# A graph attention layer and a routed feed-forward layer on one core: the attention row of the edge loops held in PSUM, and the dense softmax of the second layer put in another order

## The chip, the cores and the metric

The kernel runs on one core of a Trainium2 chip. The metric is the device time of one execution in microseconds. The profile is of one execution; its engines are TensorE (PE, with its weight loads as PEld), VectorE (DVE), ScalarE (ACT), GpSimd (POOL) and the queue of SyncE (SPq), which issues most plain DMAs.

## The reference

There are N = 625 nodes with 768 features and 10,625 edges. After a layer norm two branches are added to x, and then a routed feed-forward layer with its own layer norm:

```
x = x + gnn(xn, src, dst) + mixer(xn)
x = x + ffn(layernorm(x))
gatv2: fs = x @ Ws + bs ; fd = x @ Wd + bd
       e = leaky_relu(fs[src] + fd[dst], 0.2) ; logits = sum(e * attn)      # per edge and head
       alpha = softmax of the logits over the edges of one dst
       out = elu(sum over edges of alpha * fs[src])
gnn:   h = layer_norm(gatv2(x) with 8 heads + x) * w + b
       layer_norm(gatv2(h) with 1 head) * lno_w + lno_b
mixer: q, k, v of 12 heads of 64 ; relu features of 256 ; num / den ; @ proj_w.T + proj_b
ffn:   sigmoid gate, top 2 of 8 experts, each silu(x w1) * (x w3) @ w2, and one shared expert
```

## The kernel before

Node rows lie in T = 5 tiles of P = 125; D = 768 is six chunks (KC) of 128 for TensorE, or two halves (HALF = 384). Edges lie in ET = 84 tiles of 128. There is no planner: each engine has its own program in `build`, the order is written out by hand, and semaphores join them.

**Stages.** First the layer norm and the products of layer 1 (`products`, drained by `products_out`), written as tables of rows to DRAM. Then edge loop 1, a dense softmax of layer 1 (`dense(0)`), the products of layer 2, edge loop 2, the dense softmax of layer 2 (`dense(1)`), the gate, the shared expert and the routed jobs.

**An edge loop** (`edges` on GpSimd, `edges_first` and `edges_second` on VectorE). For tile t GpSimd issues three indirect DMAs: it gathers the rows of fs for tile t+5 (`gather_src`, L571) and of fd (`gather_dst`, L577) into a ring of G = 5 slots, and scatters the logits of tile t into a dense matrix in DRAM (`scatter`, L582). It waits for `edge_done` of tile t before the three. VectorE adds the two gathered rows (`edge_sum`, L998, 769 or 776 columns), multiplies relu of the sum by the attention row `rows[:, 2, :]`, which lies in SBUF (`weigh`, L1010 in loop 1, L1039 in loop 2), sums it and adds the linear part (`total`, L1019 and L1044, which gives `edge_done`). Loop 1 also makes one-hot rows (`hot`, L1005) and sums by head with a reduction (L1014); TensorE counts edges with them into banks 0 to 6 of PSUM (L1492). In loop 2 TensorE and ScalarE work on the mixer (`MIX_STEPS`), whose kv products use banks 4 and 5, its num products banks 6 and 7 (`mix_bank`), and the rest banks 0 to 3. From tile 64 of loop 2 on VectorE puts one step of the mixer's projection behind each tile (`project`): five divisions (L1061), two weight splits (`weights_lo`, L916), five low halves of transposes (`transposed_lo(2, t)`, L911) and ten drains of products 8 and 9 (L927). When the five transposes are done, SyncE loads x once more into `b1` (L478).

**The dense softmax of layer 2.** SyncE loads the logits of the five tiles; VectorE finds the maxima, ScalarE takes Exp, VectorE multiplies by the edge counts (`probs`). TensorE transposes each tile of probabilities (L1513), ScalarE copies it out (L738), TensorE multiplies it with fs (L1527, 20 matmuls a tile, into banks 4 and 5 or 6 and 7). Then VectorE does for one tile after another: scale (L1160), min (L1169), max (L1174), the sum with Exp from ScalarE (L746, L1185), and `finish(c)`: statistics (L888, L890), 1/std (L894, behind the square root of ScalarE, L660), two instructions for the norm's rows (L902, L904), the sum with the residual `x2` (L1208), statistics again, and the normalised tile `xf` (L898) for the gate. `transposes(3, t)` brings xf to TensorE (L1454), L668 and L911 split it in a high and a low half, `gate_product(t)` is 18 matmuls (L1436 to L1438). `x2` had got its `x` in five additions (L1146), behind which `xagain_used` lets SyncE load the first expert pieces.

Of the kernel before, what the change touches and what calls it, by code (L numbers as in the profile page):

```python
# [66 lines left out]
def build(nc, x, src, dst, W1s, b1s, W1d, b1d, attn1, ln1_w, ln1_b, Wos, bos, Wod, bod, attno, lno_w,  # L67
          lno_b, qkv_wT, qk_bcols, v_brow, proj_wT, proj_b, proj_matT, gate_wT, gate_bias, moe_w, out):
    ctx = ExitStack()
    with ctx:  # L70
# [200 lines left out]
        xagain_loaded, xagain_used = sem("xagain_loaded"), sem("xagain_used")  # L271
# [90 lines left out]
        AGG_LAG, COPY_LAG, NORM_LAG, ELU_LAG, OUT_LAG = 2, (3, 0), (4, 2), (5, 2), (6, 2)  # L362
# [6 lines left out]
        def _(sp):  # L369
# [123 lines left out]
            sp.wait_ge(xagain_used, 1)  # L493
# [155 lines left out]
        def _(act):  # L649
# [60 lines left out]
            def dense(l):  # L710
# [14 lines left out]

                if l == 1:
                    for u in range(T):
                        exps(u)
                for u in range(H * T + OUT_LAG[l] + (2 if l == 0 else 0)):
                    if l == 0 and u < H * T:  # L730
                        exps(u)
                    v = u - COPY_LAG[l]
                    if 0 <= v < H * T:
                        act.wait_ge(pt_full[l], v + 1)
                        if v >= PT_SLOTS:
                            act.wait_ge(agg_full[l], v - PT_SLOTS + 1)
                        m = v % PT_SLOTS
                        act.copy(pt[:, m * N:(m + 1) * N], pt_psum(v)).then_inc(pt_copied[l], 1)  # L738
                    if l == 0 and v == H * T - 1:
                        weights_hi([4])  # L740
                        transposed_hi(1, 0)
                    c, rest = divmod(u - ELU_LAG[l] + 1, H)
                    if rest == 0 and 1 <= c <= T:
                        elu_m = (elu_m_t, elu_m2)[l][:, :]
                        act.wait_ge(elu_min[l], c)
                        act.activation(elu_m, elu_m, ACT.Exp).then_inc(elu_exp[l], 1)  # L746
                        if l == 1:
                            ln_sqrt(2, c - 1)
                            if c >= 3:
                                transposed_hi(3, c - 3)  # L750
                            ln_sqrt(3, c - 1)
                        elif c == T:
                            transposed_hi(1, 1)
                    c, rest = divmod(u - OUT_LAG[l], H)
                    if l == 0 and rest == 0 and 1 <= c <= T:
                        ln_sqrt(1, c - 1)
# [14 lines left out]
            for n, (kind, r, h, i) in enumerate(MIX_STEPS):  # L771
# [23 lines left out]
                else:  # L795
                    last = act.copy(mix_out[:, :, 2 * r + h, :], ps[0:P, b, 0:T * (MD + 1)].rearrange("p (t d) -> p t d", t=T))
# [79 lines left out]
        def _(dve):  # L876
# [123 lines left out]
            def edges_first():  # L1000
# [63 lines left out]
            def project(i):  # L1064
# [18 lines left out]
            def dense(l, dest):  # L1083
                H = HL[l]
                DH = D // H
                elu_o, elu_m = (elu_o_t[:, :], elu_m_t[:, :]) if l == 0 else (elu_o2[:, :], elu_m2[:, :])
# [44 lines left out]
                for u in range(H * T + OUT_LAG[l] + (2 if l == 0 else 0)):  # L1131
                    if l == 0 and u < H * T:
# [8 lines left out]
                    if l == 1 and u == 0:  # L1141
                        dve.memset(at[:, :, :, N:TP].bitcast(F32), 0.0)
                        dve.wait_ge(xagain_loaded, 16 * len(PARTS))
                        dve.wait_ge(mm_used, 50)
                        for t in range(T):
                            last = dve.tensor_tensor(x2[:, t, :], x2[:, t, :], b1[:, t, :], ALU.add)  # L1146
                        last.then_inc(xagain_used, 1)
                        dve.wait_ge(xagain_used, 1)
                    c, rest = divmod(u - NORM_LAG[l] + 1, H)
                    if l == 0 and rest == 0 and c == T:  # L1150
                        weights_lo([4])
                    if rest == 0 and 1 <= c <= T:
# [6 lines left out]
                        if H == 1:  # L1159
                            last = dve.tensor_scalar(elu_o.rearrange("p (a d) -> p a d", a=2), pv, rden[:, c, 0:1], None, ALU.mult)  # L1160
                        else:
                            for b in range(2):
                                last = dve.tensor_tensor(
                                    elu_o[:, b * HALF:(b + 1) * HALF].rearrange("p (h d) -> p h d", d=DH),
                                    pv[:, b, :].rearrange("p (h d) -> p h d", d=DH),
                                    rden[:, c, 4 * b:4 * b + 4].unsqueeze(2).to_broadcast([P, 4, DH]), ALU.mult)
# [3 lines left out]
                        if l == 0:  # L1170
# [647 lines left out]
```

## Time and profile before

| | us |
|---|---|
| median of 3 runs | 1414.26 (1414.21 to 1416.88) |
| the profiled execution | 1414.86 |
| its span (first to last instruction) | 1413.1 |
| DVE busy | 943.8 (67%) |
| PE busy | 1024.6 (73%) |
| POOL busy | 619.8 (44%) |
| ACT busy | 564.1 (40%) |
| mean granted TensorE clock | 0.859 |

The span is the profiled execution less 1.8 us ahead of its first and behind its last instruction. The shares of busy time are means over stages of very different kinds, so what an engine's share says of a stage has to be read in that stage. A DMA-issuing instruction of POOL is shown with the time that it takes to be issued, not with the time of the transfer.

### The profile page before, as it was taken

Reading aid. Unit: us, or ns where it says so; the run is one execution under the profiler, and the core shown is the slowest. Engines: PE = TensorE matmul, PEld = TensorE weight load, DVE = VectorE, ACT = ScalarE, POOL = GpSimd, SP = SyncE. Lnnn points to the kernel's source line nnn. Section 1 sums busy time; section 2 is a strip of 40 time slices with the busy share of each in tenths; the row PEclk is TensorE's granted clock in tenths of the full one; section 3 lists DMA queues with packets and bytes.
Section 4 is the critical chain, followed back from the end, with each engine's and each line's share of the span. In section 5 each row is a group of like instructions: output and inputs, shape, how many; then the busy total and the mean of one; then the engine's idle time right before and its main releaser. Section 6 shows DMA issues by size and latency. Waiting matters only on the chain.

```text
span 1413.1 us, 15862 instructions
## 1 busy us (share of the span) xinstructions
PE 1024.6 (73%) x5499; PEld 855.4 (61%) x5499; DVE 943.8 (67%) x1678; ACT 564.1 (40%) x735; POOL 619.8 (44%) x581
## 2 busy tenths in 40 slices
PE   5974455545551777798999999518267998999991
PEld 5963333333331676797777778418245997888881
DVE  6548777778774787544444444475488655999993
ACT  3314333333422788310444343310034423777770
POOL 0037777777772000004777777787400000333330
PEclk9999787677875788899999999858687799999995
DMA  9856666666666550237777766758412125999986
GB/s 337 344 190 185 200 196 197 199 200 195 196 193 175 140 137 25 72 103 252 220 220 219 231 183 185 256 164 236 127 71 66 57 101 222 388 408 403 400 353 186
DMA packets 85033, 290.85 MB, mean 206 GB/s; under 512 B 15970, under 2 KB 37768, under 8 KB 84341
## 3 DMA queue, kind: packets, MB, share of 16 engines
q0 software_dynamic: 34656, 145.11, 34.3%
q1 hardware_dynamic: 46822, 130.71, 27.1%
q10 hardware_dynamic: 3488, 14.16, 2.5%
q8 instruction: 40, 0.66, 0.2%
q14 instruction: 27, 0.22, 0.1%
HBM read 258.31 MB, written 31.62 MB: 205 GB/s over the span
## 4 chain that ended last, share of the span: by engine, by line
POOL 30%; PE 29%; DVE 13%; issue 12%; DMA 12%; ACT 4%; SPq 1%; DVEq 0%; ACTq 0%; POOLq 0%
POOL dense_logits L582 11%; POOL ring_s L571 10%; POOL ring_d L577 9%; PE ps L1436 9%; PE ps L1437 9%; PE ps L1438 9%; DMA ring_d<-table_dst,dst_i 7%; ACT de L724 2%; DVE ring_s L998 2%; DVE ring_s L1010 1%; DMA dl_b<-dense_logits 1%; DVE stats L888 1%; DMA y_in<-y_rows 1%; PE ps L1527 1%; DMA dl_a<-dense_logits 1%
## 5 line engine op out<-in xcount | busy, mean ns | idle before, releaser
L998 DVE TENSOR_TENSOR ring_s<-ring_s,ring_d 128x776 f32<-128x776 f32 (+1 forms) x168 | 162.1, 965 | 255.9 <-DMA ring_d<-table_dst,dst_i 255.9
L571 POOL DMA_INDIRECT ring_s<-table_src,src_i x168 | 173.6, 1033 | 328.0 <-DVE fd_stage L927 268.7
L1492 PE MATMUL ps<-hot_s,hot_d 128*125 128x512 f16 (+1 forms) x840 | 177.7, 374 | 163.3 <-DVE hot_s L1005 162.9
L1492 PEld LDWEIGHTS ps<-hot_s,hot_d 128*125 128x125 f16 x840 | 112.0, 173 | 229.2 <-DVE hot_s L1005 173.4
L582 POOL DMA_INDIRECT dense_logits<-logits,cell_i x168 | 204.4, 1217 | 51.4 <-issue 50.6
L577 POOL DMA_INDIRECT ring_d<-table_dst,dst_i x168 | 171.4, 1020 | 76.6 <-issue 50.6
L698 ACT ACTIVATE hot_d<-iota_h,dst_bias 128x626 f16<-128x626 f16 x84 | 68.5, 816 | 220.4 <-PE ps L1492 220.3
L610 POOL COPY gather_i<-lst 128x1 int32 (+1 forms) x16 | 7.4, 463 | 245.0 <-DVE lst L1356 149.9
L1436 PE MATMUL ps<-wp,at 128*125 128x384 f32 x300 | 105.3, 351 | 11.1 <-DVE xt L927 4.1
L1437 PE MATMUL ps<-wp,at 128*125 128x384 f32 x300 | 104.0, 347 | 0.0
L1438 PE MATMUL ps<-wp,at 128*125 128x384 f32 x300 | 103.6, 345 | 0.0
L1243 DVE TENSOR_TENSOR we<-eraw,we 128x1536 fp32r<-128x1536 f32 x50 | 86.4, 1756 | 12.7 <-ACT we L814 11.8
L1527 PE MATMUL ps<-fs,dpt 125*125 125x96 f32 (+1 forms) x500 | 92.9, 342 | 0.0
L1527 PEld LDWEIGHTS ps<-fs,dpt 125*125 125x125 f32 x500 | 75.3, 216 | 13.5 <-issue 2.5
L1568 PE MATMUL ps<-xt,mix_w 128*128 128x313 f32 (+1 forms) x288 | 80.3, 436 | 2.0 <-issue 1.7
L1039 DVE SCALAR_TENSOR_TENSOR ring_d<-ring_s,rows 128x768 f32<-128x768 f32 x84 | 80.7, 961 | 0.0
L1014 DVE TENSOR_REDUCE head_sum<-ring_s 128x8 f32<-128x768 f32 x84 | 80.1, 953 | 0.0
L1010 DVE SCALAR_TENSOR_TENSOR ring_s<-ring_s,rows 128x768 f32<-128x768 f32 x84 | 80.0, 952 | 0.0
L1513 PE MATMUL ps<-ident,de 125*125 125x125 f32 x200 | 37.6, 330 | 55.5 <-DVE den L1118 34.4
L1243 DVE TENSOR_TENSOR we<-raw,we 128x1536 fp32r<-128x1536 f32 x44 | 75.8, 1752 | 0.0
L814 ACT CAST we<-eraw 128x1536 fp32r<-128x1536 f32 x50 | 72.2, 1481 | 5.6 <-PE ps L1438 5.6
L1568 PEld LDWEIGHTS ps<-xt,mix_w 128*128 128x128 f32 x288 | 54.6, 192 | 27.6 <-ACT mix_qp L769 5.2
(248 smaller groups left out, 2341.9 us busy)
## 6 DMA issues: line engine op xcount, KB each, us to landing
eraw<-in_moe_w_dram SPq DMA_DIRECT2D x50, 768.0 KB, 6.7
raw<-in_moe_w_dram SPq DMA_DIRECT2D x44, 768.0 KB, 7.3
dense_logits<-neg ACTq DMA_DIRECT2D x1, 12288.0 KB, 44.5
mix_w<-in_qkv_wT_dram SPq DMA_DIRECT2D x18, 384.0 KB, 6.1
dl_a<-dense_logits SPq DMA_DIRECT2D x2, 2187.5 KB
dl_b<-dense_logits SPq DMA_DIRECT2D x2, 2187.5 KB
y_in<-y_rows SPq DMA_DIRECT2D x5, 672.0 KB
ring_s<-table_src,src_i POOLq DMA_INDIRECT x168, 4.2
```

The source lines that it names most:

```text
L571: pool.indirect_dma_start(out=ring_s[:, j, 0:WL[l]], out_offset=None, in_=table_src[l], in_offset=bass.IndirectOffsetOnAxis(ap=src_i[:, t: ...
L577: pool.indirect_dma_start(out=ring_d[:, j, 0:WL[l]], out_offset=None, in_=table_dst[l], in_offset=bass.IndirectOffsetOnAxis(ap=dst_i[:, t: ...
L582: pool.indirect_dma_start(out=dense_logits[l], out_offset=bass.IndirectOffsetOnAxis(ap=cell_i[:, t:t + 1], axis=0), in_=logits[:, t, 0:HL[ ...
L998: dve.tensor_tensor(ring_s[:, j, 0:WL[l]], ring_s[:, j, 0:WL[l]], ring_d[:, j, 0:WL[l]], ALU.add).then_inc(z_ready[l], 1)
L1010: dve.scalar_tensor_tensor(out=v, in0=v, scalar=0.0, in1=rows[:, 2, :], op0=ALU.max, op1=ALU.mult).then_inc(mul_ready[0], 1)
L1243: dve.tensor_tensor(we[:, 2 * m + 1, part], src, we[:, 2 * m, part].bitcast(F32), ALU.subtract).then_inc(up_lo if q < 4 else w2_lo, 1)
L1436: pe.matmul(o, lt(0), r(0), start=start, stop=False)
L1437: pe.matmul(o, lt(0), r(1), start=False, stop=False)
L1438: return pe.matmul(o, lt(1), r(0), start=False, stop=stop)
L1492: last = pe.matmul(ps[0:P, b, o:o + s1 - s0], hot_d[:, j, c * P:(c + 1) * P], hot_s[:, j, s0:s1], start=start and (n <= 5 or n == 9), stop ...
L1527: last = pe.matmul(o, pt[:, m * N + s * P:m * N + (s + 1) * P], fs[:, s, col:col + w], start=s == 0, stop=s == T - 1)
L1568: last = pe.matmul(ps[:, b, 0:c1 - c0], mix_w[:, 1 - m, k, s * 128:(s + 1) * 128], xt_v[:, k, c0:c1], start=k == 0, stop=k == KC - 1)
```

## The change

1. The attention row times 0.8 is written to PSUM (`att_ps`, the last 768 columns of banks 6 and 7). In loop 1 only its last 512 columns, in bank 7, are used from there, and `weigh` is two instructions, of 256 columns (attention in SBUF) and of 512 (attention in PSUM). In loop 2 the whole row is read from PSUM by the one `weigh`.
2. Banks 6 and 7 are no longer used by the mixer: its num products go to other columns of the banks of kv (`NUM_AT`), and the transposes of stage 2 use banks 4 and 5 only: `transposes(2, t)` now waits for the low half of tile t-1, where it waited for t-2.
3. The second addition of x is gone. The two biases (proj_b, lno_b) are added by TensorE, two matmuls of one row ahead of each product of q = 8 and 9, and the drain adds `b1` (x loaded again) in place of a bias row; it waits for `xagain_loaded`. SyncE loads the first expert pieces when `mm_used` is 50.
4. The dense softmax of layer 2 has loops of its own: ScalarE makes max(scale*v, 0) from PSUM, VectorE the min in one instruction, and VectorE works on tile c and on the norms of tile c-1 in turn. Per tile it issues one scale-and-min, one sum, two instructions for the norm and the residual (before: two and one more), the two statistics, two reciprocals and the normalisation. `transposed_lo(3, t)` is three rounds behind; `copy_probs(4)` of ScalarE stands behind Exp of tile 0 and ahead of that tile's square root.

```diff
+        att_ps = ps[:, 6:8, :].rearrange("p a b -> p (a b)")[:, 1024 - D:1024]
-                b = (0 if n == 3 else 4) + 2 * (t % 2)
+                b = 2 * (t % 2) if n == 3 else 4
...
-            sp.wait_ge(xagain_used, 1)
+            sp.wait_ge(mm_used, 50)
...
+                    for v in range(PT_SLOTS):
+                        copy_probs(v)
+                    for c in range(T + 1):
+                        if c < T:
+                            act.wait_ge(elu_min[l], c + 1)
+                            pv = ps[0:P, 4 + 2 * (c % 2):6 + 2 * (c % 2), 0:HALF]
+                            act.activation(elu_o2[:, :].rearrange("p (a d) -> p a d", a=2), pv, ACT.Relu,
+                                           scale=rden[:, c, 0:1]).then_inc(elu_max[l], 1)
+                            act.activation(elu_m2[:, :], elu_m2[:, :], ACT.Exp).then_inc(elu_exp[l], 1)
+                        if c == 0:
+                            copy_probs(PT_SLOTS)
+                        if c >= 3:
+                            transposed_hi(3, c - 3)
+                        if c >= 1:
+                            ln_sqrt(3, c - 1)
+                        if c < T:
+                            ln_sqrt(2, c)
...
-                dve.tensor_scalar(rows[:, 2, :], rows[:, 2, :], 0.8, None, ALU.mult).then_inc(att_scaled, 1)
+                if l == 0:
+                    dve.tensor_scalar(att_ps[:, D - 512:D], rows[:, 2, D - 512:D], 0.8, None, ALU.mult)
+                    dve.tensor_scalar(rows[:, 2, 0:D - 512], rows[:, 2, 0:D - 512], 0.8, None, ALU.mult).then_inc(att_scaled, 1)
+                else:
+                    dve.tensor_scalar(att_ps, rows[:, 2, :], 0.8, None, ALU.mult).then_inc(att_scaled, 1)
...
-                    v = ring_s[:, t % G, 0:D]
-                    dve.scalar_tensor_tensor(out=v, in0=v, scalar=0.0, in1=rows[:, 2, :], op0=ALU.max, op1=ALU.mult).then_inc(mul_ready[0], 1)
+                    for cols, att in ((slice(0, D - 512), rows[:, 2, 0:D - 512]), (slice(D - 512, D), att_ps[:, D - 512:D])):
+                        v = ring_s[:, t % G, cols]
+                        last = dve.scalar_tensor_tensor(out=v, in0=v, scalar=0.0, in1=att, op0=ALU.max, op1=ALU.mult)
+                    last.then_inc(mul_ready[0], 1)
...
-                    dve.scalar_tensor_tensor(out=ring_d[:, j, 0:D], in0=ring_s[:, j, 0:D], scalar=0.0, in1=rows[:, 2, :],
+                    dve.scalar_tensor_tensor(out=ring_d[:, j, 0:D], in0=ring_s[:, j, 0:D], scalar=0.0, in1=att_ps,
...
-                    products_out(8 + q, x2, 3, "proj", tiles=(t,))
+                    dve.wait_ge(xagain_loaded, 16 * len(PARTS))
+                    u = 5 * (8 + q) + t
+                    dve.wait_ge(mm_full, u + 1)
+                    dve.tensor_tensor(x2[:, t, q * HALF:(q + 1) * HALF], ps[0:P, u % 4, 0:HALF],
+                                      b1[:, t, q * HALF:(q + 1) * HALF], ALU.add).then_inc(mm_used, 1)
...
+                for c in range(T + 1):
+                    if c < T:
+                        dve.wait_ge(agg_full[1], c + 1)
+                        pv = ps[0:P, 4 + 2 * (c % 2):6 + 2 * (c % 2), 0:HALF]
+                        dve.tensor_scalar(elu_m2[:, :].rearrange("p (a d) -> p a d", a=2), pv, rden[:, c, 0:1], 0.0,
+                                          ALU.mult, ALU.min).then_inc(elu_min[1], 1)
+                    if c >= 1:
+                        o = gnn[:, c - 1, :]
+                        ln_rstd(2, c - 1)
+                        after(dve.scalar_tensor_tensor(out=o, in0=o, scalar=mv[:, c - 1, 0:1], in1=rows[0:P, 0, :],
+                                                       op0=ALU.subtract, op1=ALU.mult))
+                        after(dve.scalar_tensor_tensor(out=x2[:, c - 1, :], in0=o, scalar=rstd[:, c - 1:c], in1=x2[:, c - 1, :],
+                                                       op0=ALU.mult, op1=ALU.add))
+                        ln_stats(c - 1, x2[:, c - 1, :])
+                    if c >= 3:
+                        transposed_lo(3, c - 3)
+                    if c < T:
+                        dve.wait_ge(elu_exp[1], c + 1)
+                        dve.wait_ge(elu_max[1], c + 1)
+                        dve.scalar_tensor_tensor(out=gnn[:, c, :], in0=elu_m2[:, :], scalar=-1.0, in1=elu_o2[:, :],
+                                                 op0=ALU.add, op1=ALU.add).then_inc(out_ready[1], 1)
+                        dve.wait_ge(out_ready[1], c + 1)
+                        ln_stats(c, gnn[:, c, :])
+                    if c >= 1:
+                        ln_rstd(3, c - 1)
+                        normalise(c - 1, x2[:, c - 1, :], xf[:, c - 1, :]).then_inc(ln_done, 1)
...
-                back = (4, 1, 2, 2)[n]
+                back = (4, 1, 1, 2)[n]
...
+                    if q >= 8:
+                        for r in (3, 1):
+                            pe.matmul(ps[0:P, u % 4, 0:HALF], ones_row[:, :], rows[0:1, r, (q - 8) * HALF:(q - 7) * HALF],
+                                      start=r == 3, stop=False)
...
+NUM_AT = 2 * (MD + 1)
-    if kind == "kv":
+    if kind in ("kv", "num"):
         return 4 + h
-    if kind == "num":
-        return 6 + h
```

## Rows read from the trace of the kernel before

**Rows 1.** Busy time by stretch: edge loop 1, edge loop 2 (columns in the row's order: stretch, length, PE, PEld, DVE, ACT, POOL, clock, DMA share, GB/s).

```profile
100.00:435.00 335.00, 176.14 (x830) 110.89 (x830) 259.56 (x417) 124.89 (x167) 257.18 (x243) 0.77 0.67 192
664.00:1010.00 346.00, 278.92 (x1566) 228.37 (x1566) 180.35 (x355) 108.61 (x237) 271.84 (x242) 0.89 0.70 207
```

**Rows 2.** Groups of POOL in loop 1, stretch 104 to 436.

```profile
L582 POOL DMA_INDIRECT dense_logits<-logits,cell_i x84 | 102.0, 1214 | 25.8 <-issue 25.0 <-DVE logits L1019 0.8
```

**Rows 3.** Groups of POOL in loop 2, stretch 664 to 1010.

```profile
L582 POOL DMA_INDIRECT dense_logits<-logits,cell_i x84 | 102.4, 1219 | 25.6 <-issue 25.6
L577 POOL DMA_INDIRECT ring_d<-table_dst,dst_i x79 | 84.9, 1074 | 24.1 <-issue 24.1
L571 POOL DMA_INDIRECT ring_s<-table_src,src_i x79 | 84.6, 1071 | 28.9 <-issue 22.3 <-DVE logits L1044 6.6
```

**Rows 4.** Timeline of loop 1 (start, length, engine, line).

```profile
205.95 0.97 DVE L998 TENSOR_TENSOR ring_s<-ring_s,ring_d 128x776 f32<-128x776 f32 x1 [1.04 <-DMA ring_d<-table_dst,dst_i]
206.44 1.33 POOL L582 DMA_INDIRECT dense_logits<-logits,cell_i  x1 [0.30 <-issue]
```

**Rows 5.** Timeline of loop 2: POOL and DVE at three places.

```profile
665.58 0.96 DVE L1039 SCALAR_TENSOR_TENSOR ring_d<-ring_s,rows 128x768 f32<-128x768 f32 x1
665.78 1.57 POOL L577 DMA_INDIRECT ring_d<-table_dst,dst_i  x1 [0.30 <-issue]
...
936.04 2.55 DVE L916 TENSOR_TENSOR wp<-wraw,wp 128x2304 fp32r<-128x2304 f32 x1
936.36 3.07 POOL L571 DMA_INDIRECT ring_s<-table_src,src_i  x1 [0.30 <-issue]
...
979.22 1.73 POOL L577 DMA_INDIRECT ring_d<-table_dst,dst_i  x1 [0.30 <-issue]
```

**Rows 6.** Groups of DVE by form in the dense softmax of layer 2, 1038 to 1097.4.

```profile
L888 DVE BATCH_NORM_STATS2 stats<-gnn 125x6 f32<-125x384 f32 x10 | 5.1, 552 | 0.2
L904 DVE SCALAR_TENSOR_TENSOR gnn<-gnn,rstd,rows 125x768 f32<-125x768 f32 x5 | 5.1, 1019 | 0.2
...
L1160 DVE TENSOR_SCALAR elu_o<-ps,rden 125x768 f32<-125x768 f32 x5 | 5.1, 1018 | 3.1 <-PE ps L1527 3.0
...
L898 DVE TENSOR_SCALAR xf<-xt,mv,rstd 125x768 f32<-125x768 f32 x5 | 3.4, 680 | 0.2
...
L894 DVE RECIPROCAL rstd<-std 125x1 f32<-125x1 f32 x10 | 1.6, 164 | 3.6 <-ACT std L660 3.6
```

**Rows 7.** Timeline from the dense softmax to the shared expert: first DVE, then PE.

```profile
1038.58 1.02 DVE L1160 TENSOR_SCALAR elu_o<-ps,rden 125x768 f32<-125x768 f32 x1 [2.96 <-PE ps L1527]
...
1045.84 6.62 PE L1527 MATMUL ps<-fs,dpt 125*125 125x384 f32 x20
1060.56 1.48 PE L1454 MATMUL ps<-ident,xf 125*128 125x125 f32 x6 [8.10 <-ACT dpt L738]
...
1084.97 1.51 PE L1454 MATMUL ps<-ident,xf 125*128 125x125 f32 x6 [6.57 <-DVE xf L898]
...
1101.82 0.37 PE L1436 MATMUL ps<-gate_w_hi,at 128*125 128x8 f32 x1 [1.86 <-DVE at L911]
...
1109.40 0.61 PE L1436 MATMUL ps<-at,we 128*128 128x314 f32 x1
```

**Rows 8.** Group of DVE whose second input lies in PSUM, whole span.

```profile
L1365 DVE TENSOR_TENSOR silu<-silu,ps 128x314 f32<-128x314 f32 x4 | 1.9, 472 | 0.0
```

**Rows 9.** Timeline near loop 2's end: last projection product, last drain.

```profile
997.16 0.34 PE L1438 MATMUL ps<-wp,at 128*125 128x384 f32 x1
...
1007.34 0.55 DVE L927 TENSOR_TENSOR xt<-ps,rows 125x384 f32<-125x384 f32 x1
```

**Rows 10.** Groups of ACT in the same stage, 1028 to 1097.

```profile
L660 ACT ACT_TABLE_LOAD x5 | 6.4, 1283 | 0.1
...
L746 ACT ACTIVATE elu_m<-elu_m 125x768 f32<-125x768 f32 x5 | 4.2, 843 | 12.9 <-DVE elu_m L1169 12.9
L738 ACT COPY dpt<-ps 125x625 f32<-125x625 f32 x5 | 3.4, 672 | 2.3 <-PE ps L1513 2.3
```

More of the change, by code:

```diff
@@ L731, in dense @@
+                    return
+                for u in range(H * T + OUT_LAG + 2):
+                    if u < H * T:
                         exps(u)
-                    v = u - COPY_LAG[l]
+                    v = u - COPY_LAG
                     if 0 <= v < H * T:
[L734 to L738, printed above, removed]
@@ L739, in dense @@
-                    if l == 0 and v == H * T - 1:
+                        copy_probs(v)
+                    if v == H * T - 1:
                         weights_hi([4])
                         transposed_hi(1, 0)
-                    c, rest = divmod(u - ELU_LAG[l] + 1, H)
+                    c, rest = divmod(u - ELU_LAG + 1, H)
                     if rest == 0 and 1 <= c <= T:
-                        elu_m = (elu_m_t, elu_m2)[l][:, :]
                         act.wait_ge(elu_min[l], c)
[L746 to L752, printed above, removed]
+                        act.activation(elu_m_t[:, :], elu_m_t[:, :], ACT.Exp).then_inc(elu_exp[l], 1)
+                        if c == T:
@@ L753, in dense @@
                             transposed_hi(1, 1)
-                    c, rest = divmod(u - OUT_LAG[l], H)
-                    if l == 0 and rest == 0 and 1 <= c <= T:
+                    c, rest = divmod(u - OUT_LAG, H)
+                    if rest == 0 and 1 <= c <= T:
                         ln_sqrt(1, c - 1)
@@ L795, in _ @@
                 else:
-                    last = act.copy(mix_out[:, :, 2 * r + h, :], ps[0:P, b, 0:T * (MD + 1)].rearrange("p (t d) -> p t d", t=T))
+                    last = act.copy(mix_out[:, :, 2 * r + h, :], ps[0:P, b, NUM_AT:NUM_AT + T * (MD + 1)].rearrange("p (t d) -> p t d", t=T))
                 last.then_inc(mix_used, 1)
@@ L1130, in dense @@
                         probs(u)
-                for u in range(H * T + OUT_LAG[l] + (2 if l == 0 else 0)):
-                    if l == 0 and u < H * T:
+                    second()
+                    return
+                for u in range(H * T + OUT_LAG + 2):
+                    if u < H * T:
                         c, h = divmod(u, H)
@@ L1140, in dense @@
                             joined(c + 1)
[L1141 to L1150, printed above, removed]
+                    c, rest = divmod(u - NORM_LAG + 1, H)
+                    if rest == 0 and c == T:
                         weights_lo([4])
@@ L1199, in dense, with second @@
                         normalise_rows(c - 1, b1[:, c - 1, :]).then_inc(ln_done, 1)
-            def finish(c):
-                o = gnn[:, c, :]
-                ln_stats(c, o)
-                ln_rstd(2, c)
-                after(normalise_rows(c, o))
-                after(dve.tensor_tensor(x2[:, c, :], x2[:, c, :], o, ALU.add))
-                if c >= 2:
-                    transposed_lo(3, c - 2)
-                ln_stats(c, x2[:, c, :])
-                ln_rstd(3, c)
-                normalise(c, x2[:, c, :], xf[:, c, :]).then_inc(ln_done, 1)
+            def second():
+                dve.wait_ge(mm_used, 50)
+                dve.memset(at[:, :, :, N:TP].bitcast(F32), 0.0)
+                dve.wait_ge(probs_ready[1], T)
+                after(dve.tensor_scalar(rden[:, :, 0:1], den[:, :, 0:1], 1e-30, None, ALU.max))
+                after(dve.reciprocal(rden[:, :, 0:1], rden[:, :, 0:1]))
+                for c in range(T + 1):
[24 more added lines that the diff above has]
+                        normalise(c - 1, x2[:, c - 1, :], xf[:, c - 1, :]).then_inc(ln_done, 1)
@@ L1215, in _ @@
             dve.wait_ge(counts_ready, 1)
-            dense(0, b1)
+            dense(0)
             for t in range(2, T):
```

70 lines of the change are left out of this document (31 added, 39 removed).

## The prediction

> **What bounds the kernel now.** I first read the busy time by stretch. In both edge loops no compute engine is full, but GpSimd issues indirect DMAs without a pause: 242 instructions take 271.8 us of loop 2, and each has about 0.30 us of issue ahead of it, 72.6 us, which together fill the 346 us; in loop 1 the same sum gives 257.2 + 72.6 = 329.8 of 335 us [rows 1]. So the reader should take GpSimd's instruction length as the loops' clock: 84 tiles with three instructions each. VectorE is 260 of 335 us busy in loop 1 and 180 of 346 in loop 2, and waits for gathers.
>
> Then I read GpSimd's groups. Loop 1's scatter has a mean of 1214 ns [rows 2], loop 2's three kinds have 1219, 1074 and 1071 ns [rows 3]; unhindered, each takes 0.94 to 0.98 us in the timeline. The excess is what can be won. The timeline of both engines side by side shows where it comes from: a scatter that starts at 206.44, while edge_sum runs from 205.95 to 206.92, takes 1.33 us; it ends some 0.9 us after edge_sum does [rows 4]. A gather that starts inside `weigh` takes 1.57 us, one that starts inside a weight split of 2.55 us takes 3.07 us [rows 5]. I put each start of GpSimd in the two loops beside the VectorE instruction that ran then. Loop 2: 28 of 242 starts fell in `weigh` (L1039), 22 were lengthened, by 14.8 us together (first at 665.78, last at 979.22 [rows 5]); 51 fell in edge_sum, 42 lengthened, 18.9 us; 5 in divisions and weight splits, 5.1 us. Loop 1: 55 in edge_sum, 21.0 us (one of them in [rows 4]); 22 in the one-hot, 1.4 us; 6 in `weigh`, only 2 lengthened, 1.7 us. 77 starts in the reduction (one SBUF input), 10 in instructions with an input in PSUM (L911, L927), and 223 with VectorE idle have no excess. So an instruction with two inputs in SBUF holds GpSimd up at its start, one with an input in PSUM does not.
>
> Last I read the dense softmax of layer 2 by VectorE's groups and TensorE's timeline. There VectorE is the bound: five tiles take it the 59.4 us of the stretch, 11.9 each, and a dependent instruction of 768 columns costs 1.02 us and 0.03 more to its successor [rows 6], while TensorE waits 8.10 and 6.57 us [rows 7].
>
> **Loop 2.** `weigh` has one SBUF input afterwards, so its 14.8 us go. Its own length hardly matters: with PSUM as second input, as here, 314 columns take 472 ns [rows 8]; scaled up in full that is 1.15 us for 768, against 0.96 now [rows 5], and VectorE is idle for half of the loop. I take 0.96, since part of the 472 ns is the same for any length. But GpSimd then comes earlier to its next starts, and some of them meet edge_sum. The bound for that is loop 1, where `weigh` hardly ever hits: edge_sum costs 21.0 us there, 2.1 more than in loop 2. So loop 2 gets 14.8 - 2.1 = 12.7 us shorter. Bounds: 17 (edge_sum's hits fall too), 5 (two thirds of the removed excess comes back as hits on edge_sum).
>
> The Trainium skill (SBUF — State Buffer, Who interferes with whom) says that a VectorE instruction with two SBUF inputs contends with a GpSimd instruction that reads SBUF, and one with at most one SBUF input, outside the two-port modes, does not; the trace agrees, 22 of 28 against 0 of 10. The same section infers that descriptor generation needs the write interface, and that tensor_tensor therefore does not stall it. By that, nothing would be won in the loops; this is a rival below, and the 3.07 us instruction speaks against it.
>
> **The tail of loop 2.** Moved work could undo this. Transposes of stage 2 go one by one: each waits for the low half that VectorE makes in the tile before, some 4 us, and needs 1.5 us of PE and 0.8 of ScalarE, so VectorE finds them ready. The last comes one tile later, and so does the load of x, on SP's queue behind nothing else; the logits' load queued behind it waits for the last scatter anyway. The drains now need that load. It is 1.9 MB, which at the 207 GB/s of [rows 1] is 9.3 us, and the first drain is two tiles (8 us) behind; VectorE's gathers are delayed meanwhile as they are before. A stall of 1 to 2 us is taken by the ring, five tiles deep. The 20 bias matmuls cost at most what a plain f32 matmul of 384 columns costs, 6.62/20 = 0.33 us [rows 7], so 6.6 us; the last product ends at 997.5, the last drain starts at 1007.3 [rows 9], so 9.8 us of cover. Taken as 0; were this cover gone, every us past it would delay the last `edge_done` and the last scatter one for one. The num products in kv's banks wait for kv products that they need in any case: 0. The scaling of the attention row to PSUM runs before the first gather lands: 0.
>
> **Loop 1.** Two instructions in place of one cost VectorE some 0.1 us a tile, of 3.1 against a period of 4.0 us (335/84): hidden, and GpSimd is behind VectorE, not ahead. Of the 1.7 us in `weigh` a third stays possible: -1.1. Shifted phases can cost or give: -3 to +3. I take -0.6.
>
> **The dense softmax of layer 2.** VectorE's steps, start to start: scale-and-min 1.05; reciprocal 0.2; two norm instructions 2.1; statistics of x2 1.3; sum 1.0; statistics 1.3; reciprocal 0.2; normalise 0.6: 7.75 us a tile, and 0.9 more with a transpose's low half [rows 6]. The waits for ScalarE, at 0.36 us each and more, are filled by the other tile. ScalarE needs per tile Relu 0.8, Exp 0.84, two table loads 2.6, two square roots 0.6 and a copy 0.8 [rows 10], 5.6 us: below VectorE. TensorE needs 6.62 + 0.8 [rows 7].
>
> Start: the first aggregation ends at 1038.5 as before [rows 7]; the five additions of x lay ahead of VectorE's wait of 2.96 us for it [rows 7], so their removal gives 0. Min at 1039.6, Exp done at 1041.4. Then a new wait: ScalarE's copy of the fifth transposed tile, which TensorE makes only between the second aggregation and the third (up to 1045.84 [rows 7]), stands ahead of tile 0's square root: copy 0.67, table load 1.28, root 0.3 give 1048.3 (1043.7 before). VectorE, ready at 1046.6, waits 1.7 us for it. Tile 0 is normalised at 1048.4 + 0.2 + 2.1 + 1.3 + 2.3 + 0.8 = 1055.1. Tile 1 at 1062.9, tile 2 at 1071.5, tile 3 at 1080.2; TensorE's aggregations, from 1055.9 and 1063.5, stay ahead of these. I put 0.3 for small waits: tile 3 at 1080.5, 4.5 us before the 1084.97 of [rows 7].
>
> From there the bound is no longer VectorE but TensorE, at the lower of its two clocks: 36 gate products take 1109.40 - 1101.82 = 7.58 us, 0.21 each [rows 7]. Behind tile 3 follow its transposes 1.5, three gate products of a tile 11.4, the transposes of tile 4 1.5, two more gate products 7.6: 22.0 us, so the gate ends at 1102.5 instead of 1109.4. The 2.4 us that it waited for low halves go, since these are made in time (the third at 1085, needed at 1089.6). So this stage gives 6.9 us, though VectorE's own chain is 11 us shorter; the rest lies in the wait for the gate. Bounds: 3 (small waits on ScalarE come back at each of five tiles) and 11 (TensorE, idle less, keeps the 2.4 GHz level through part of the 90 gate products). Everything later hangs on the gate. The earlier load of the first expert pieces, behind the logits in the same queue, is hidden: 0.
>
> **Sum.** 12.7 + 0.6 + 6.9 = 20.2 us, from the profiled execution's own 1414.86: 1394.7; the median lies 0.6 lower, so 1394.1.
>
> **The rivals.**
> Both gains as above: 0.58, between 1388 and 1401.
> The loops give little: GpSimd's starts that no longer meet `weigh` meet edge_sum, as 42 of 51 starts in it are lengthened. For: its landing time ties edge_sum to GpSimd's own rhythm. Against: loop 1, where the tie exists and costs 0.25 us a tile. With the loops at -3: 1404. Chance 0.12. With it goes the port rule's other reading (no gain in the loops at all, 1407): 0.04.
> The dense stage gives nothing: its waits move to ScalarE, whose copy, Relu, Exp and roots now stand in one fixed order. Against: 5.6 of 7.75 us. 1401: 0.10.
> More than forecast: clock in the gate and all 17 us of loop 2: 1385. Chance 0.11.
> Slower: VectorE becomes the bound of loop 1. The split `weigh` reads PSUM in each of 84 tiles, and if the pair cost more than 0.9 us over the present 0.95, a tile would pass the 4.0 us period; from 1.15 us over, 84 x 0.25 = 21 us would eat all gains; at 1.4 it gives 1415. Against: [rows 8]. Chance 0.03. Other small or no change 0.02.
>
> **Range.** From 1383 (the larger gains) to 1406 (one of the two gains missing). The likeliest case alone: 1388 to 1401. 0.2% (2.8 us) is about what a measurement of this kernel can tell from no change. Faster by more than that 0.94, within it 0.03, slower 0.03.
>
> **What would show it.** Right: GpSimd's mean in loop 2 falls from 1071 to 1220 ns towards 1.02 to 1.2, no start inside L1039's successor is lengthened, loop 2 is about 12 us shorter and loop 1 unchanged; the last tile's drains wait for nothing; in the dense stage VectorE needs some 7.8 to 8.7 us a tile, tile 0's reciprocal waits some 1.7 us for ScalarE, and the gate ends 22 us behind tile 3. Wrong: more starts in edge_sum than 55 a loop; VectorE waiting for x in the tail; ScalarE as the releaser in each dense tile; another granted clock in the gate.

## The result, and the profile after

The changed kernel takes 1407.5 us (median of 10 runs, 1402.3 to 1408.6) against 1414.2 for the kernel before, run beside it on the same chip: ratio 0.9951, 95% interval 0.9931 to 0.9971. It is faster, by 6.7 us; forecast were 20.2 us, so the time lies above the range that ended at 1406. The profiled execution took 1408.08 us (span 1406.3), 6.8 less than the one before, so it can be read for the difference. Two executions of all those below ran at a much lower granted clock (1690 us at 0.60, 1448 us at 0.76) and are in no ratio.

Read in order of time, as distances to the trace of before: the last scatter of loop 1 ends 0.5 us earlier (434.52), that of loop 2 only 2.1 us (1007.70 against 1009.76), the gate 9.1 us (1100.67), the kernel's last write 6.8 us. So the dense stage gave 7.0 us, and nearly all that is missing is missing in loop 2. The last 2.3 us between gate and end prove nothing: a second profile of the kernel before against the first has -2.6 at the gate and -0.1 at the end, and over the fourteen profiles of this case that stretch takes 303 to 308 us, whichever kernel it is. The 0.5 us of loop 1 prove nothing either: it ends at 432.32 in the second profile of the kernel before.

Loop 2 on GpSimd (groups of instructions, 664 to 1010; answers to [rows 3]):

```profile
L584 POOL DMA_INDIRECT dense_logits<-logits,cell_i x84 | 97.2, 1157 | 30.9 <-issue 24.7 <-DVE logits L1067 6.2
L573 POOL DMA_INDIRECT ring_s<-table_src,src_i x79 | 82.6, 1045 | 33.9 <-issue 22.3 <-DVE logits L1067 11.7
L579 POOL DMA_INDIRECT ring_d<-table_dst,dst_i x79 | 79.0, 1000 | 24.1 <-issue 24.1
```

The busy sum fell from 272 to 259 us, by 13.1 where 12.7 were forecast. The idle column grew: 17.9 us of idle time are put down to VectorE's logits, 6.6 before. The removed stalls are there; new waits stand beside them. GpSimd's timeline shows where:

```profile
969.84 0.98 POOL L584 DMA_INDIRECT dense_logits<-logits,cell_i  x1 [0.30 <-issue]
975.52 0.97 POOL L573 DMA_INDIRECT ring_s<-table_src,src_i  x1 [4.70 <-DVE logits L1067]
...
1002.79 0.96 POOL L584 DMA_INDIRECT dense_logits<-logits,cell_i  x1 [2.87 <-DVE logits L1067]
1006.75 0.95 POOL L584 DMA_INDIRECT dense_logits<-logits,cell_i  x1 [3.00 <-DVE logits L1067]
```

Less the usual 0.30 each, that is 9.7 us, all in the last 40 us of the loop. As the loop also starts later, its first gather by 0.8 us and its first logits by another 0.6, -13.1 + 9.7 + 1.4 = -2.0: the whole of the 2.1. VectorE's groups of the same stretch and its waits near the end name what it waited for:

```profile
L1062 DVE SCALAR_TENSOR_TENSOR ring_d<-ring_s,ps 128x768 f32<-128x768 f32 x83 | 79.2, 954 | 0.0
...
L1105 DVE TENSOR_TENSOR xt<-ps,b 125x384 f32<-125x384 f32 x10 | 5.6, 556 | 22.3 <-DMA b<-in_x_dram 11.6 <-PE ps L1465 10.6
```

```profile
973.75 0.56 DVE L1105 TENSOR_TENSOR xt<-ps,b 125x384 f32<-125x384 f32 x1 [11.64 <-DMA b<-in_x_dram]
...
991.32 0.56 DVE L1105 TENSOR_TENSOR xt<-ps,b 125x384 f32<-125x384 f32 x1 [2.42 <-PE ps L1465]
...
996.18 0.56 DVE L1105 TENSOR_TENSOR xt<-ps,b 125x384 f32<-125x384 f32 x1 [2.43 <-PE ps L1465]
...
1001.02 0.56 DVE L1105 TENSOR_TENSOR xt<-ps,b 125x384 f32<-125x384 f32 x1 [2.42 <-PE ps L1465]
...
1005.85 0.56 DVE L1105 TENSOR_TENSOR xt<-ps,b 125x384 f32<-125x384 f32 x1 [2.41 <-PE ps L1465]
```

First a wait of 11.64 us for x, then four drains, 4.84 us apart, that wait for TensorE; before, the drains waited for nothing, and the last was at 1007.34 [rows 9]. `weigh` itself takes 954 ns with the row in PSUM (961 with both inputs in SBUF). The load of x is issued here:

```profile
953.80 0.88 SPq L480 DMA_DIRECT2D b<-in_x_dram  x2
```

and TensorE's side of the drains is this:

```profile
966.97 1.55 PE L1494 MATMUL ps<-rows,ones_row 1*125 1x384 f32 x4
968.45 0.44 PE L1463 MATMUL ps<-wp,at 128*125 128x384 f32 x1
...
971.55 0.34 PE L1465 MATMUL ps<-wp,at 128*125 128x384 f32 x1
971.82 0.91 PE L1494 MATMUL ps<-rows,ones_row 1*125 1x384 f32 x2
```

x was issued at 953.80 and used at 973.75: 20 us for 1.9 MB, not 9.3. The DMA engines were full meanwhile. The busy time of that stretch, and below it that of the same load in the trace of the kernel before, where it was issued at 958.27 and its last packet ended at 973.1 (columns as in [rows 1], DMA share and GB/s last):

```profile
953.80:973.70 19.90, 19.90 (x72) 14.95 (x73) 4.38 (x9) 2.20 (x3) 13.19 (x13) 0.81 0.96 250
```

```profile
958.30:973.10 14.80, 13.64 (x72) 13.32 (x71) 5.54 (x10) 2.18 (x3) 11.75 (x11) 0.93 1.01 254
```

The load already took 15 us there; nobody waited for it.

The two bias matmuls of a product are four records and take 1.48 us from the first's start to the next matmul, at the 2.4 GHz level (granted clock 1.00 from 964 to 974); eighteen others take the remaining 3.36 of a product's 4.84 us. From the start of the first product (953.70) to the end of the last (1005.75) TensorE does not wait once.

The dense stage, first VectorE's timeline, then TensorE's (to be read beside [rows 7]):

```profile
1036.40 1.02 DVE L1219 TENSOR_SCALAR elu_m<-ps,rden 125x768 f32<-125x768 f32 x1 [7.06 <-PE ps L1558]
...
1046.18 0.16 DVE L911 RECIPROCAL rstd<-std 125x1 f32<-125x1 f32 x1 [1.84 <-ACT std L662]
...
1069.71 0.68 DVE L915 TENSOR_SCALAR xf<-xt,mv,rstd 125x768 f32<-125x768 f32 x1
...
1078.28 0.68 DVE L915 TENSOR_SCALAR xf<-xt,mv,rstd 125x768 f32<-125x768 f32 x1
...
1100.67 0.18 DVE L1285 TENSOR_SCALAR gate_s<-gate_s 125x40 f32<-125x40 f32 x1 [1.98 <-ACT gate_s L841]
```

```profile
1079.02 1.51 PE L1481 MATMUL ps<-ident,xf 125*128 125x125 f32 x6 [7.71 <-DVE xf L915]
...
1091.53 1.51 PE L1481 MATMUL ps<-ident,xf 125*128 125x125 f32 x6
```

Tiles 2 and 3 are 8.57 us apart (12.1 before), tile 0's square root is waited for, and the gate ends 21.7 us behind tile 3 (from the end of its normalisation).

### The profile page after: what moved, and what is told of

It reads as the page before. It is cut to its first block, busy times and chain, and to the rows that moved or that the text cites. A ratio compares the mean times of both kernels' runs of the same rounds, so it can differ in the third digit from the quotient of the medians.

```text
span 1406.3 us, 15997 instructions
## 1 busy us (share of the span) xinstructions
PE 1048.8 (75%) x5539; PEld 869.4 (62%) x5539; DVE 933.2 (66%) x1735; ACT 569.7 (41%) x740; POOL 605.4 (43%) x581
## 4 chain that ended last, share of the span: by engine, by line
PE 35%; POOL 30%; issue 12%; DMA 9%; DVE 8%; ACT 4%; SPq 1%; DVEq 0%; ACTq 0%; POOLq 0%
POOL dense_logits L584 11%; PE ps L1463 10%; POOL ring_s L573 10%; PE ps L1464 10%; PE ps L1465 10%; POOL ring_d L579 9%; DMA ring_d<-table_dst,dst_i 4%; PE ps L1558 2%; ACT de L726 2%; PE ps L1494 1%; DMA dl_b<-dense_logits 1%; DMA y_in<-y_rows 1%; DMA dl_a<-dense_logits 1%; DVE ring_s L1019 1%; PE ps L1544 1%
## 5 line engine op out<-in xcount | busy, mean ns | idle before, releaser
L584 POOL DMA_INDIRECT dense_logits<-logits,cell_i x168 | 198.0, 1178 | 56.7 <-issue 49.9
L579 POOL DMA_INDIRECT ring_d<-table_dst,dst_i x168 | 165.3, 984 | 76.4 <-issue 50.6
L1062 DVE SCALAR_TENSOR_TENSOR ring_d<-ring_s,ps 128x768 f32<-128x768 f32 x84 | 80.1, 954 | 0.0
L1463 PE MATMUL ps<-we,atg 128*128 128x512 f32 x168 | 68.1, 405 | 3.9 <-issue 1.9
```

The costliest lines, as they stand in the source:

```text
L579: pool.indirect_dma_start(out=ring_d[:, j, 0:WL[l]], out_offset=None, in_=table_dst[l], in_offset=bass.IndirectOffsetOnAxis(ap=dst_i[:, t: ...
L584: pool.indirect_dma_start(out=dense_logits[l], out_offset=bass.IndirectOffsetOnAxis(ap=cell_i[:, t:t + 1], axis=0), in_=logits[:, t, 0:HL[ ...
L1463: pe.matmul(o, lt(0), r(0), start=start, stop=False)
```

## The experiments

All ratios are against the kernel before, run beside each. Twelve kernels in three sets; the kernel before had medians of 1412.5, 1411.2 and 1412.2 us in them. Each ratio is uncertain by 0.2 to 0.3%, 3 to 4 us, so a difference between two of the kernels below is uncertain by 4 to 5 us, and medians and ratios can give it 2 to 3 us apart.

**One bias row instead of two** (theory: TensorE's bias matmuls; rival: the load of x). VectorE adds the two rows once.

```diff
+                    dve.tensor_tensor(rows[0:1, 3, :], rows[0:1, 3, :], rows[0:1, 1, :], ALU.add).then_inc(bias_summed, 1)
-                        for r in (3, 1):
-                            pe.matmul(ps[0:P, u % 4, 0:HALF], ones_row[:, :], rows[0:1, r, (q - 8) * HALF:(q - 7) * HALF],
+                        pe.matmul(ps[0:P, u % 4, 0:HALF], ones_row[:, :], rows[0:1, 3, (q - 8) * HALF:(q - 7) * HALF],
```

> The changed kernel with the two bias rows summed once by VectorE, so that TensorE adds one bias row per projection product and not two. Theory (A: TensorE's pace in the tail of edge loop 2 ate part of the gain): a product takes about 4.84 - 0.78 = 4.07 us, about the period of an edge tile; GpSimd's two last gaps (2.87 and 3.0 us) fall to 0.3 to 1, the gap of 4.7 us where VectorE waits for x stays. Loop 2 ends 3 to 5.5 us earlier: 1402 to 1404.5 against the changed kernel's 1407.5. Rival (B: only the wait for x costs, TensorE has cover): no change, 1407.5.

1403.0 us, ratio 0.9924 (0.9904 to 0.9943), in the expected range. TensorE's products are 4.2 us apart, and VectorE, late after its wait for x, never waits for one:

```profile
963.22 0.91 PE L1497 MATMUL ps<-rows,ones_row 1*125 1x384 f32 x2
967.41 0.91 PE L1497 MATMUL ps<-rows,ones_row 1*125 1x384 f32 x2
971.62 0.91 PE L1497 MATMUL ps<-rows,ones_row 1*125 1x384 f32 x2
```

GpSimd's one gap left is that of x (its timeline, then VectorE's):

```profile
976.97 0.97 POOL L574 DMA_INDIRECT ring_s<-table_src,src_i  x1 [3.98 <-DVE logits L1068]
```

```profile
975.20 0.56 DVE L1109 TENSOR_TENSOR xt<-ps,b 125x384 f32<-125x384 f32 x1 [10.94 <-DMA b<-in_x_dram]
```

**x loaded tile by tile** (theory: removing the wait for x alone gives nothing, since TensorE's pace stands behind it; rival: it gives the 4.4 us of the gap). SP waits for each tile's transposes and loads that tile, each drain waits for its own tile.

```diff
-            sp.wait_ge(tr_full, 3 * T)
-            for a, b in PARTS:
-                sp.dma_start(b1[a:b, :, :], x.rearrange("(t p) d -> p t d", p=P)[a:b, :, :]).then_inc(xagain_loaded, 16)
+            for t in range(T):
+                sp.wait_ge(tr_full, 2 * T + t + 1)
+                for a, b in PARTS:
+                    sp.dma_start(b1[a:b, t, :], x[t * P + a:t * P + b, :]).then_inc(x_loaded[t], 16)
```

> The changed kernel with x loaded again tile by tile, each tile as soon as its own transposes are done, and the drains waiting for their own tile only. The two bias matmuls stay. Theory A: the gap of 4.7 us in GpSimd goes, but TensorE's products run without a pause from 953.7 to 1005.4 us in the changed kernel whether VectorE waits or not, so the last gaps grow by as much (to 4 to 6 us in three or four places together about 10) and the loop ends where it did: 1406 to 1408. Rival B: 4.4 us faster, 1403.

1406.5 us, ratio 0.9948 (0.9927 to 0.9969): nothing gained over the changed kernel that the runs could tell. No instruction waits for x any more, every drain waits for TensorE (4.74 us the first, 2.4 each other), and GpSimd's gaps at the end are 2.8, 3.9, 3.9 and 3.0 us, 12.4 less the usual 0.30 each. This profile is of the slowest of the six executions (1411.9 us).

```profile
1000.14 0.56 DVE L1106 TENSOR_TENSOR xt<-ps,b 125x384 f32<-125x384 f32 x1 [2.43 <-PE ps L1466]
1004.98 0.56 DVE L1106 TENSOR_TENSOR xt<-ps,b 125x384 f32<-125x384 f32 x1 [2.42 <-PE ps L1466]
1009.82 0.56 DVE L1106 TENSOR_TENSOR xt<-ps,b 125x384 f32<-125x384 f32 x1 [2.41 <-PE ps L1466]
```

**Both together.**

> Both edits: one bias row and x tile by tile. Theory A: GpSimd has no gap above 1 us in the tail of loop 2, the loop ends 8 to 10 us earlier than in the changed kernel: 1398 to 1400. Rival B: 1403, as with x alone. Rival C (the give-back is elsewhere, in the gate or the jobs): 1406 or more.

1400.4 us, ratio 0.9907 (0.9886 to 0.9928), just above the expected 1398 to 1400. Products every 4.2 us, gaps of 1.18 and 2.36 us at the end where none above 1 was expected: one bias matmul per product is still too much.

**Neither load nor bias** (x by tile; this kernel leaves both bias rows out of the output).

> The changed kernel with x loaded tile by tile and without any bias product on TensorE. It leaves out the addition of the two bias rows (proj_b and lno_b) from the output. It measures the price of the two bias matmuls by itself: a product is 3.28 us, below the 4 us of an edge tile, so GpSimd has no gap above 0.3 us in the tail. Theory: 9 to 10.5 us faster than the changed kernel, 1397 to 1398.5. Rival (the kernel with one bias row and x by tile has won all there is): 1400.

1397.8 us, ratio 0.9896 (0.987 to 0.9923). No drain waits, no gap of GpSimd is left. That is what the changed kernel would take if its tail cost nothing. First and last matmul of TensorE's ten products, and the last drain:

```profile
954.18 0.67 PE L1464 MATMUL ps<-wp,at 128*125 128x384 f32 x1
...
987.75 0.34 PE L1466 MATMUL ps<-wp,at 128*125 128x384 f32 x1
```

```profile
995.95 0.55 DVE L1106 TENSOR_TENSOR xt<-ps,b 125x384 f32<-125x384 f32 x1
```

The ten products take 33.9 us here and 52.05 us in the changed kernel, so the bias matmuls cost TensorE 18.1 us in all; and the last product ends 7.9 us ahead of the last drain, which is the cover that the changed loop really has.

**The attention row alone** (the kernel before with only the loops' part, without the mixer's biases and x and without the dense stage), twice, the second time 2 sets later.

> The kernel before with the attention row in PSUM alone, as in parts 1 and 2 of the change (mixer on six banks, transposes of stage 2 one by one); biases, residual and dense softmax as before. Theory: GpSimd's instructions in loop 2 sum to 259 us and not 272, no gap in the tail, so 12 to 13.5 us off: 1401 to 1402.5. Rival (the transposes one by one hold VectorE up in the tail, not the biases): 4 to 10 us of gaps, 1405 to 1410.

> The attention row in PSUM alone on the kernel before, once more. Its first profile showed 12.7 us less in loop 2, its first median 6.4 us less than the kernel before. Theory (the profiles' sums are typical): 10 to 12 us less than the kernel before. Rival (they lie at the ends of the spread: before's profiled execution was one of its slower ones): 6 to 8 us less, with GpSimd's sum in loop 2 between 258 and 263 us.

1406.1 us, ratio 0.9954 (0.9932 to 0.9976), and 1401.7, 0.9921 (0.9888 to 0.9953). The first misses its expectation of 12 us or more by half: 6.4 us; the second gives 10.5. In both profiles GpSimd's sum in loop 2 is 259 and 257 us, and no gap is in the tail: with the transposes one by one but without the bias matmuls and the wait for x, nothing is given back there. The end of loop 2 comes 13 and 15 us earlier. The medians say 6 to 10; the first profiled execution took 1402.9 us, 3.2 less than its kernel's median, the second 1399.7, 2.0 less, and that of the kernel before 1414.9, some 2 more than its medians here.

**The attention row back in SBUF, all else as changed.**

> The changed kernel with the attention row back in SBUF in both loops; everything else of the change stays. Theory: GpSimd's instructions in loop 2 sum to 270 to 273 us again (259 in the changed kernel), with some 20 starts in weigh lengthened. The tail is still paced by TensorE, whose products start when VectorE reaches tile 72, which is about 11 us later; so the loop ends 9 to 12 us later than in the changed kernel: 1416 to 1419, a little slower than before, though the dense softmax is 7 us shorter. Rival (the port does not matter, the gain came from the dense softmax alone): 1407.5, no change.

1413.6 us, ratio 1.0004 (0.998 to 1.0028); 1416 to 1419 were expected, so the row is worth less than was expected of it here too. All of the gain is gone, though from the end of loop 2 to the gate it is still 9.1 us shorter than before: loop 2 itself takes 6.2 us more than before, 5.5 of it in gaps of GpSimd in the tail. In GpSimd's timeline, starts inside `weigh` are lengthened again (VectorE first, then GpSimd):

```profile
666.80 0.96 DVE L1059 SCALAR_TENSOR_TENSOR ring_d<-ring_s,rows 128x768 f32<-128x768 f32 x1
```

```profile
667.05 1.56 POOL L573 DMA_INDIRECT ring_s<-table_src,src_i  x1 [0.30 <-DVE logits L1064]
```

By count, 25 of 30 starts in `weigh` are lengthened, by 16.8 us together; in the changed kernel 0 of 20. Each lengthened start, here and in the kernel before, ends 0.81 to 0.86 us behind the end of the VectorE instruction that it met.

**The same without biases and with x by tile** (leaves both bias rows out of the output), so that no tail hides the difference.

> As the kernel without bias products and with x by tile (it too leaves the two bias rows out of the output), but with the attention row back in SBUF in both loops. Beside e6_no_bias_x_by_tile (1397.8) it gives the worth of the attention row in PSUM where nothing in the tail takes it back; beside the kernel before, the worth of the dense softmax alone. Theory: GpSimd's instructions in loop 2 sum to 272 us, no gap in the tail, dense stage 7 us shorter than before: 1404 to 1407, 7 to 9 us above e6. If the single profiles overstate the loop's gain, 3 to 6 us above e6.

1405.2 us, ratio 0.9935 (0.9911 to 0.9959); 7.4 us slower by the median than with the row in PSUM, 5.5 by the ratios of the two sets, which does not tell the two cases of the expectation apart. Its GpSimd sum is 268.3 us (272 expected), with 18 starts in `weigh`, 13 lengthened by 8.3 us. Against the kernel before, what is left here is the dense stage: 7.0 us by the medians.

**The dense stage's own two waits** (theory: tile 0's 1.8 us and the low-clock gate products behind tile 3 are both order, not work). ScalarE's copy of the fifth transposed tile goes behind tile 0's square root, and two gate products go ahead of tile 3's transposes.

```diff
-                        if c == 0:
-                            copy_probs(PT_SLOTS)
                         if c >= 3:
                             transposed_hi(3, c - 3)
                         if c >= 1:
                             ln_sqrt(3, c - 1)
                         if c < T:
                             ln_sqrt(2, c)
+                        if c == 0:
+                            copy_probs(PT_SLOTS)
...
-            transposes(3, 3, xf)
...
-            for t in range(3):
-                gate_product(t)
+            gate_product(0)
+            gate_product(1)
+            transposes(3, 3, xf)
+            gate_product(2)
```

> The changed kernel with the two edits of the dense stage alone (the copy of the fifth transposed tile behind tile 0's square root; gate products of tiles 0 and 1 ahead of tile 3's transposes). Theory: VectorE's wait of 1.84 us at tile 0 goes, the gate ends 3 to 5.5 us earlier relative to the end of loop 2: 1402 to 1404.5. Rival: the gate's end is held by the split of the expert pieces on ScalarE, 1406.

1400.2 us, ratio 0.9924 (0.9901 to 0.9946): better than the 1402 to 1404.5 expected. Over the changed kernel that is 6 to 7 us by the medians and 3 to 4 by the ratios. From the end of loop 2 to the gate the stage is now 14.6 us shorter than before, not 7.0; without these two edits that stretch is 7 to 9 us shorter in eight profiles.

```profile
1043.38 0.15 DVE L911 RECIPROCAL rstd<-std 125x1 f32<-125x1 f32 x1
...
1092.50 0.18 DVE L1285 TENSOR_SCALAR gate_s<-gate_s 125x40 f32<-125x40 f32 x1 [4.38 <-ACT gate_s L841]
```

**The version that this points to.** x by tile, the summed bias row split into a rounded and a remaining part for two single-pass matmuls, and the two edits of the dense stage.

```diff
+                    dve.tensor_tensor(rows[0:1, 3, :], rows[0:1, 3, :], rows[0:1, 1, :], ALU.add).then_inc(bias_summed, 1)
...
+                    dve.tensor_copy(bias_r[:, 0, :], rows[0:1, 3, :]).then_inc(bias_summed, 1)
...
+                    dve.tensor_tensor(bias_r[:, 1, :], rows[0:1, 3, :], bias_r[:, 0, :].bitcast(F32), ALU.subtract).then_inc(bias_split, 1)
```

> A version to beat both: x tile by tile, the summed bias row split in a high and a low half so that its two matmuls are single-pass (0.17 us each instead of 0.39 twice for each of two rows), the copy of the fifth transposed tile behind tile 0's square root, and the gate products of tiles 0 and 1 ahead of the transposes of tile 3. Theory: the tail without gaps gives 9 to 10.5 us, the copy 1.8 at tile 0, the gate 3 to 4: 13 to 15 us faster than the changed kernel, 1392.5 to 1395. Rival (TensorE's clock falls further in the gate, or the copy then delays the fourth aggregation): 1397 or more.

1393.3 us (1390.8 to 1395.0), ratio 0.9866 (0.984 to 0.9892), the fastest here. Products are 3.9 us apart (4.84 in the changed kernel), and GpSimd's last gaps are 0.85 and 2.10 us.

**Both kernels again.**

> The changed kernel on the chip of these comparisons: 6 to 8 us less than the kernel before, gaps of 8 to 10 us in the tail of loop 2 again (waits for x and for TensorE).

> The kernel before itself, for a second profile: GpSimd's sum in loop 2 near 272 us if the first profile was typical, 265 to 268 if it was an extreme. Time equal to the kernel before.

The changed kernel: 1406.2 us, ratio 0.9944 (0.9924 to 0.9965), with GpSimd gaps of 3.36, 2.64, 3.89 and 3.00 us in the tail: 11.7 us given back, where gaps of 8 to 10 were expected. The kernel before as its own comparison: ratio 1.0 (0.9977 to 1.0023), 1407.6 to 1418.1. A single execution of one kernel can lie 5 us and more from its median, so single profiles bear out where time is lost, and medians how much.

## Why the prediction was wrong

**The step that failed** is the one headed "The tail of loop 2", "Taken as 0". It cost 9.7 us of GpSimd's time in the profile (11.7 in the second one). Three sizes in it were wrong, and the prediction had named the sign of it: VectorE waiting for x in the tail.

The bias matmuls: "20 bias matmuls cost at most what a plain f32 matmul of 384 columns costs, 6.62/20 = 0.33 us". The row read had `x20` for ten matmuls (five tiles of source rows, two halves): a plain f32 matmul stands in this trace as two records, as the bias pair's `x4` shows. The "20 matmuls a tile" of the section on the kernel before is the same slip. By that row a matmul costs 0.66 us; a bias matmul takes 0.74, half of the pair's 1.48, so 20 take 14.8 us. By the difference between the two runs of ten products they cost TensorE 18.1 us in all, not 6.6; the first pair alone takes 2.85 us, as the granted clock is 0.62 from 954 to 964.

The cover: "so 9.8 us of cover", read in the kernel before. Without bias matmuls the changed loop has 7.9 us. The same transposes one by one that the step mentions let the products start about a tile later, and that was not taken off; no run isolates it, but the kernel without biases and with the row in SBUF, at the old pace of the loop, has 7.8 too. 18.1 less 7.9 is 10.2 us, against 9.7 and 11.7 us given back in the two profiles. So the rule of the forecast, one for one beyond the cover, holds with the measured sizes; with 14.8 and 9.8 it would have given only 5.0.

The load of x: "at the 207 GB/s of [rows 1] is 9.3 us" and "a stall of 1 to 2 us is taken by the ring". The load took 20 us; the drain that needed it stood 8.3 us behind the issue, as forecast, and so waited 11.64 us, of which the ring took some 7 and GpSimd lost 4.4. The rate of the stretch was not free for it: the gathers already make up those 207 GB/s, and with the load beside them the DMA engines were busy to 0.96 at 250 GB/s in all. The trace of the kernel before had this load, with 15 us, to be read.

The two losses do not add up. TensorE runs its ten products without a pause whether VectorE waits for x or not, and so its pace sets the end of the loop: tile-wise x alone gives nothing, one bias row alone gives 4.5 us over the changed kernel, both 7, no biases 9.7 (each by its median against 1407.5, across sets; 0, 4, 6 and 8 by the ratios). The wait for x costs something only where the bias is cheaper: 3.7 us of gap with one bias row. So TensorE's bias work was the larger cause, which the first two experiments tell apart.

**Loop 2's gain** was right in the profile (-13.1 against -12.7): no start in `weigh` is lengthened, and what starts in edge_sum lose rose from 18.9 to 20.3 us, 1.4 where 2.1 were allowed. The Trainium skill (SBUF — State Buffer, Who interferes with whom) has the contention as one between VectorE instructions with two SBUF inputs and GpSimd instructions that read SBUF; the trace agrees, 22 of 28 against 0 of 20. The same section infers that tensor_tensor does not stall descriptor generation; that fails here, as 42 of 51 starts in edge_sum, a TENSOR_TENSOR with both inputs in SBUF, were lengthened. But in medians the row in PSUM is worth 6.4, 10.5, 7.4 and, in the presence of the tail, 6.1 us, some 7.6 on average and not 12.7 (by the ratios 6.5, 11.2, 5.5 and 7.5). Each is clear of zero, and 12.7 lies above the interval of all but the second. The profiles' sums for the kernels with the row in SBUF are 272.1, 271.5, 272.8 and 268.3 us, with it in PSUM 257.4 to 263.3. How many starts fall into `weigh` (15 to 32) changes from execution to execution, and I take it to hang on the phase of two engines. That the medians of the loop-only kernel stay under its profiles is in part the choice of executions: the profiled ones were 3.2 and 2.0 us faster than their medians, that of the kernel before some 2 slower. Whether a favourable phase made them fast was not settled.

**Loop 1** came out as forecast, -0.5 against -0.6, but that is no evidence: two profiles of the kernel before differ by 2.7 us there. VectorE's busy time there grew from 259.6 to 266.1 us, 0.08 us a tile, hidden.

**The dense stage** was right: 7.0 (6.9), 7 to 9 in eight profiles; tile 0's reciprocal waits 1.84 us for ScalarE (1.7); tiles 8.6 us apart with a low half (7.75 + 0.9); the gate ends 21.7 us behind tile 3 (22.0). Only tile 2 came later than forecast, 10.5 us behind tile 1 where 8.6 were: TensorE's aggregation took 8.31 us at a granted clock of 0.79, and VectorE waited 1.82 us for it; in the kernel with one bias row it took 6.62 us at 1.00. TensorE's gate products set the end, as said; the two edits above show that as much again was still in the order, 7.5 us in their profile.

**The range** did not hold the time because this zero had no bound in it: no rival had the tail's cost. With the 9.7 us of the profile in its place and 12.7 kept, the sum would have been 1403.8, inside the range; with the loops' 7.6 us of the medians as well, 1408.9, against 1407.5 measured. So the tail is what failed, and the size of loop 2's gain, as far as the medians can tell, took the rest.

## What to carry to other kernels

Before a moved matmul is called covered, count its records: look up in a row with a known number of matmuls how many records one makes and what it costs from start to start; and take off the cover whatever the same change makes start later. A load put beside a stage that keeps the DMA engines busy can get half of the mean rate, so place it by its own measured time, which may stand in the trace before, or cut it into pieces that can start earlier; and where a term is taken as zero for its cover, write down what the cover minus a doubled cost would be. A gain on the engine that sets a loop's pace is only worth what the work moved into that loop's tail leaves of it.

## What the runs showed of the hardware

A one-row f32 matmul of 384 columns costs TensorE 0.74 us from start to start, no less than one of 125 rows (ten in 6.62 us, both at a granted clock of 1.00), and each shows as two records. With the two rows summed, rounded and split into two single-pass matmuls a product takes 3.9 us in place of 4.84. Reading one input from PSUM costs VectorE nothing in `weigh`: 954 against 961 ns. GpSimd's instruction for an indirect DMA, when it starts during edge_sum or `weigh` with both inputs in SBUF and is lengthened, ends 0.80 to 0.86 us behind the end of that VectorE instruction, so 0.95 us becomes up to 1.77; one that starts in the first 0.02 us is not lengthened, and one in the last 0.1 us loses nothing. With the second input of `weigh` in PSUM none was lengthened, in ten profiles with 15 to 32 such starts each. A 1.9 MB load in loop 2's tail took 20 us (15 in the kernel before), where the stretch's mean rate would have made it 9; the DMA engines were then busy to 0.96 and 1.01 of the time, 0.71 and 0.70 over the loop.
